# Building the one-hot picks of a GNN kernel on GpSimd, one chunk at a time behind the gathers

## The reference

```python
h_self = x @ W_self.T + b_self
messages = x[src] @ W_neigh.T + b_neigh
h_neigh = segment_sum(messages, dst, num_segments=50000)
out = layernorm(x + relu(h_self + h_neigh))      # over the last axis, eps 1e-5
```

## Time and profile before

| | us |
|---|---|
| median of three runs | 678.21 (675.71 to 680.98) |
| profiled execution, its time | 679.41 |
| its span, first to last instruction | 677.6 |
| DVE busy / of it picks | 420.5 / 104.9 |
| POOL busy / of it the 391 gathers | 406.4 / 382.0 |
| PE busy | 512.6 |
| mean granted clock of TensorE | 0.917 |

### The profile page before, as it was taken

How to read it: one execution, slowest core, us unless ns; L and a number is a source line. 1 busy time by engine, 2 the same in 40 slices (tenths; PEclk the granted TensorE clock), 3 DMA queues, 4 the chain that set the end, 5 groups by cost and what they waited for, 6 DMA issues and landing times.

```text
span 677.6 us, 12705 instructions
## 1 busy us (share of the span) xinstructions
PE 512.6 (76%) x3281; PEld 466.3 (69%) x3281; DVE 420.5 (62%) x1921; ACT 352.7 (52%) x1049; POOL 406.4 (60%) x424
## 2 busy tenths in 40 slices
PE   2045866887977978976977796978887878889883
PEld 0034756787867968866866696967776767778872
DVE  7884757587667677877557745445545543655554
ACT  1010354465655654654665655555655555656567
POOL 4776755666666665765666566566666666656610
PEclk9999897897997788999898988899999799889798
DMA  2522243354553563544544545444555454445433
GB/s 78 144 64 52 80 114 94 102 142 123 141 143 92 151 170 97 151 123 112 139 124 123 149 123 135 115 133 115 139 134 138 114 137 131 122 137 136 135 103 96
DMA packets 122942, 82.20 MB, mean 121 GB/s; under 512 B 15374, under 2 KB 115894, under 8 KB 122840
## 3 DMA queue, kind: packets, MB, share of 16 engines
q1 hardware_dynamic: 109208, 53.63, 28.4%
q0 software_dynamic: 13664, 27.77, 16.4%
HBM read 55.44 MB, written 26.71 MB: 121 GB/s over the span
## 4 chain that ended last, share of the span: by engine, by line
PE 50%; issue 20%; ACT 12%; another core or an unknown queue 6%; DVE 4%; DMA 3%; ACTq 2%; SPq 2%; POOL 1%; DVEq 0%
PE bank L890 17%; PE bank L913 11%; PE bank L914 9%; PE bank L878 6%; ACT result L1024 6%; PE bank L909 3%; ACT sums_t L997 3%; PE bank L895 3%; ACT x_t L1005 2%; DMA x_in<-in_x 2%; ACT std L1014 1%; ACTq L995 1%; DVE y L741 1%; DVE pick L731 1%
## 5 line engine op out<-in xcount | busy, mean ns | idle before, releaser
L483 POOL DMA_INDIRECT ring<-in_x,chunk_src x391 | 382.0, 977 | 229.9 <-issue 85.2
L741 DVE SCALAR_TENSOR_TENSOR y<-bank,x_in 128x384 f32<-128x384 f32 x131 | 72.5, 554 | 233.2 <-remote 114.5
L997 ACT COPY sums_t<-bank 128x192 f32 x391 | 125.2, 320 | 168.9 <-issue 45.0
L890 PE MATMUL bank<-pick,ring 128*128 128x193 f32 (+1 forms) x782 | 188.9, 370 | 10.6 <-DMA ring<-in_x,chunk_src 6.3
L913 PE MATMUL bank<-wsum_t,x_t 128*128 128x128 f32 (+1 forms) x782 | 175.7, 307 | 3.6 <-issue 3.6
L914 PE MATMUL bank<-wn_t,sums_t 128*128 128x128 f32 (+1 forms) x782 | 162.0, 290 | 7.1 <-issue 7.0
L1024 ACT ACTIVATE result<-y,minus_mean,rstd 128x128 f32<-128x128 f32 x391 | 162.9, 482 | 0.0
L890 PEld LDWEIGHTS bank<-pick,ring 128*128 128x128 f32 x782 | 142.2, 216 | 13.0 <-issue 12.7
L913 PEld LDWEIGHTS bank<-wsum_t,x_t 128*128 128x128 f32 (+1 forms) x782 | 126.8, 203 | 29.1 <-issue 29.0
L878 PE MATMUL bank<-identity,x_in 128*128 128x128 f32 x391 | 74.2, 304 | 92.5 <-issue 46.4
L914 PEld LDWEIGHTS bank<-wn_t,sums_t 128*128 128x128 f32 (+1 forms) x782 | 128.3, 206 | 8.5 <-issue 8.5
(11 more groups left out here) (118 smaller groups left out, 175.1 us busy)
## 6 DMA issues: line engine op xcount, KB each, us to landing
x_in<-in_x SPq DMA_DIRECT2D x130, 192.0 KB
out<-result SPq DMA_DIRECT2D x130, 192.0 KB
ring<-in_x,chunk_src POOLq DMA_INDIRECT x391
degrees_t<-degrees_dram SPq DMA_DIRECT2D x130, 2.2 KB
dst_padded<-in_dst SPq DMA_DIRECT2D x1, 390.6 KB
src_padded<-in_src SPq DMA_DIRECT2D x1, 390.6 KB
edge_src<-in_src SPq DMA_DIRECT2D x1, 390.6 KB
edge_dst<-in_dst SPq DMA_DIRECT2D x1, 390.6 KB
```

What stands on the lines that cost most here:

```text
L483: nc.gpsimd.indirect_dma_start(ring[:, c % RING, :], None, x, bass.IndirectOffsetOnAxis(ap=chunk_src[:, c:c + 1], axis=0)).then_inc(gather ...
L741: v.scalar_tensor_tensor(y[tau % DEEP][0:rows, 0:tiles, :], h_bank[b][0:rows, 0:tiles * DIM].rearrange("p (q d) -> p q d", q=tiles), 0.0, ...
L890: ins = mm(into[:, frame:frame + SPAN + carried], ring[:, c % RING, :], pick[tau % DEEP][:, c % TRIO, 0:SPAN + carried], start=(c == 0), s ...
L997: nc.scalar.copy(sums_t[:, bass.ds(at, SPAN)], sum_bank[c // PAIR % SUM_BANKS][:, frame:frame + SPAN]).then_inc(sums_placed, 1)
```

## The change

The picks move from DVE to POOL. POOL builds pick c - 1 right after it has issued gather c, and the last one behind the last gather. The buffers become a ring of 12 single picks, and pick c has the same place in it as its rows have in `ring`, so the wait of a gather for its place frees both. `pick_built` now counts chunks instead of trios, and PE waits for it before each chunk. A pick needs `local`, so DVE counts `locals_known` up where it finishes a part of it, and POOL waits for that. On DVE `build_picks` and its calls are gone; the three portions of the first degrees, which stood between the early picks, follow each other.

```diff
-    pick = [sb(f"pick{i}", [P, TRIO, SPAN + 2]) for i in range(DEEP)]
+    pick = sb("pick", [P, RING, SPAN + 2])
...
-            pool.wait_ge(chunks_known, 1)
-            for c in range(SPREAD):
+            def build_pick(c):
+
+                pool.wait_ge(locals_known, min((c + 1) // SPREAD, 2) + 1)
+                nc.gpsimd.tensor_scalar(pick[:, c % RING, :], columns[:], local[:, c:c + 1], None, ALU.is_equal).then_inc(pick_built, 1)
+
+            for c in range(CHUNKS):
+                if c == 0:
+                    pool.wait_ge(chunks_known, 1)
+                if c == SPREAD:
+                    pool.wait_ge(chunks_known, 3)
+                if c == 2 * SPREAD:
+                    pool.wait_ge(chunks_known, 5)
                 gather(c)
-            pool.wait_ge(chunks_known, 3)
-            for c in range(SPREAD, 2 * SPREAD):
-                gather(c)
-            pool.wait_ge(chunks_known, 5)
-            for c in range(2 * SPREAD, CHUNKS):
-                gather(c)
-
+                if c >= 1:
+                    build_pick(c - 1)
+            build_pick(CHUNKS - 1)
...
-                link(v.scalar_tensor_tensor(local[:, r0:r1], carry[:, r0:r1], float(SPAN), local[:, r0:r1], ALU.mult, ALU.max))
+                v.scalar_tensor_tensor(local[:, r0:r1], carry[:, r0:r1], float(SPAN), local[:, r0:r1], ALU.mult, ALU.max).then_inc(locals_known, 1)
...
-            def build_picks(tau):
-
-                if tau >= DEEP:
-                    dve.wait_ge(chunks_summed, TRIO * (tau - DEEP + 1))
-                for c in chunks_of(tau):
-                    ins = v.tensor_scalar(pick[tau % DEEP][:, c % TRIO, :], columns[:], local[:, c:c + 1], None, ALU.is_equal)
-                ins.then_inc(pick_built, 1)
...
-            build_picks(0)
             degrees_start(0, 1)
-            degrees_bits(0, 1, range(0, 3))
-            build_picks(1)
-            degrees_bits(0, 1, range(3, 6))
-            build_picks(2)
-            degrees_bits(0, 1, range(6, SHIFT_BITS))
+            degrees_bits(0, 1, range(0, SHIFT_BITS))
             degrees_end(0, 1)
-            built = 3
...
-                while built * TRIO < sums_ahead(t + 1):
-                    build_picks(built)
-                    built += 1
...
+                pe.wait_ge(pick_built, c + 1)
                 if c % TRIO == 0:
-                    pe.wait_ge(pick_built, tau + 1)
                     pe.wait_ge(gathered[tau % GATHER_SEMS], gathers_upto(tau))
...
-                ins = mm(into[:, frame:frame + SPAN + carried], ring[:, c % RING, :], pick[tau % DEEP][:, c % TRIO, 0:SPAN + carried],
+                ins = mm(into[:, frame:frame + SPAN + carried], ring[:, c % RING, :], pick[:, c % RING, 0:SPAN + carried],
```

## The result

| | before | after |
|---|---|---|
| median of four runs, us | 678.9 | 867.8 |
| ratio after / before | | 1.275 (1.271 to 1.279) |
| profiled execution's span, us | 677.6 | 866.6 |
| first and last gather start, us | 38.1, 648.6 | 38.4, 841.5 |
| mean step from gather to gather, us | 1.565 | 2.059 |

The kernel became 27.5% slower. I had forecast 719 us, 6% slower, with a range that ended at 775. The direction came out, and so did the mechanism, that POOL becomes the pace; the size did not.

The account below looks back on a forecast made before the run. It took PE, ACT and DVE's loop as the pace, POOL close behind. POOL's step became 1.26 + 0.43 = 1.69 us; 38.1 + 659.1 + 2.9 + 18.2 = 718.3, then + 1.8 - 1.2 = 719 us, range 672 to 775.

Parts of the forecast that it names:

- The 0.29 us a chunk: POOL's true waiting for a full ring of 12, about 112 us in all, taken as all the room POOL has.
- The line 59.8 + 390 steps: Total time in us: 59.8 for start, landing, tail and median's offset, plus 390 POOL steps from gather to gather.
- The start: Time before the first gather on POOL, expected to stay at 38.1 us.
- DVE's relief: Removing 391 picks, 104.9 us of DVE busy time; credited at 0, at best some us.
- the price x of a pick on POOL: Time one pick adds to POOL's step behind each gather: 0.43 us, the middle of 0.26 and 0.62.
- The upper bound: Highest price of a pick on POOL: DVE's 0.324 us plus a second 0.30 us gap, 0.62 us.
- Rival 4: Pick on POOL costs over 0.55 us, by double hand-over or slower compare; 793 us at 0.62; chance 0.13.
- The bound from below: Lowest price of a pick on POOL, from iota over the same 128x194: about 0.26 us.
- the gather gets shorter: POOL's gather with its gap falls from 1.277 to 1.26 us, half of 12 us of stretching credited.
- the loop of PE, ACT and DVE: Said to set the mean pace before the change, a little slower than POOL's 1.28 us a chunk.
- (2): Pick fits into the 0.30 us gap behind each POOL gather, costing 0 to 0.15 us: 675 to 682 us; chance 0.15.
- (3): DVE was part of the pace-setting loop, so removing its picks makes the kernel faster: 653 to 670 us; chance 0.10.

Follow-up runs that it names:

- `e2_no_picks`: Kernel before, with DVE building only the picks of the first six trios, reused for all later chunks: 678.8 us, ratio 0.998.
- `e4_third`: Kernel before, with POOL building the third pick of each trio of chunks and DVE the other two: 678.2 us, ratio 0.998.
- `e1_pool_load`: Kernel before, all picks still on DVE, with POOL doing the same instruction behind each gather into a ring nobody reads: 874.7 us, ratio 1.287.
- the zoo: Kernel before plus one spare POOL instruction behind each gather, another form every 30 chunks; only durations count, e.g. tensor_scalar 0.325 us at two columns.
- `e5_no_gathers`: Kernel before, with no gathers after the first 12 chunks and no PE waits for later rows: 528.0 us, ratio 0.786.

## Why the prediction was wrong

**Right: what POOL has room for.** The 0.29 us a chunk was read from the gathers' rate and the waits. A third of the picks (0.27 us) and the memset (0.14 us) cost nothing; half of them (0.4 us) made it 7% slower.

**Right: POOL becomes the pace, and where to look.** Ring waits fell from 144 to 8 us, gathers came evenly, and POOL rose to 87% (I said 78). DVE fell to 346 us busy, where I had subtracted the picks in full and said 315. The line 59.8 + 390 steps gives 863 us with the measured step of 2.059, against 868. The start held. Behind the last gather came 25.1 us (841.5 to 866.6) where I had 21.1, because the last sum came 7.7 us after it and not 2.9.

**Right: DVE's relief is worth 0**, in `e2_no_picks` and `e4_third`. Where POOL sets the pace it may be worth a little: with the picks still on DVE (`e1_pool_load`) POOL's step was 2.073 us and not 2.059, 5 us over 390 steps, hardly more than the noise.

**Wrong, the step that failed: the price x of a pick on POOL.** I took 0.43 us between bounds of 0.26 and 0.62. It is 2.059 - 1.26 = 0.80 us, so 390 x 0.37 = 144 us of the 149 that I missed by. The upper bound was no bound. It was DVE's 0.324 us plus a second gap of 0.30, as if POOL could not be slower at the arithmetic than DVE; but the gap did not double (0.04 + 0.17 us in all, less than the one gap of before), and POOL needs 2.6 times as long as DVE for the instruction (828 against 324 ns). Rival 4, "a dear pick", is what came true: x over 0.55, "by a compare that goes slower than DVE's". I gave it 0.13 and followed it only to x = 0.62 and 793 us, so the range was cut on the side where it mattered. The bound from below came from iota, which writes and does not read, and the zoo shows that it says nothing of `tensor_scalar`: same engine, same shape, 0.317 against 0.8 us.

The estimate by the Trainium skill (GPSIMD Engine Reference, section 3.1) fell with it: 0.42 us by about 1.8 cycles an element. The trace disagrees; 2.7 ns a column is 3.2 cycles at 1.2 GHz, and 0.3 us is fixed. Its advice in section 4.1, elementwise work to VectorE, is what this case bears out, and it spoke for the slow side of my range.

**Wrong: the gather gets shorter.** I credited 1.277 to 1.26 us for DVE's picks gone. It had 0.04 us in front of the pick, 1.03 us and 0.17: with its gaps 1.24, so the sum held by chance, with a longer gather and shorter gaps than I thought.

**Wrong, without effect on the sum: the loop of PE, ACT and DVE sets the pace before.** It ran at 528 us alone. What I called a pause that "comes from the PE/ACT/DVE loop" needs the indirect DMAs, at about one each 1.57 us, whether or not PE uses them and however few bytes they carry. A wait named "PE" is a wait for PE's signal, not proof that PE's own work is the limit.

**The rivals.** That the pick fits into the 0.30 us gap (2) was wrong by the timeline: POOL's step grew by the whole of the pick. DVE in the loop (3) was wrong by `e2_no_picks`.

## What to carry to other kernels

Work that is moved to another engine is priced by the same kind of instruction on that engine; if the trace has none, a row of another kind bounds it from below at best, and the range must reach to several times the price on the old engine (here 2.6 times). Before that, count the room of the receiving engine as its rate and not as its busy share: here it was 0.29 us of 1.565, and 0.8 us went in. And relief is worth something only on an engine that someone waits for: DVE without its picks brought 0.

## What the runs showed of the hardware

- **Indirect DMAs from POOL that follow each other closely go with late signals of PE.** At one each 1.54 to 1.57 us, PE's records run on while ACT, DVE and POOL get its increments some us late and all together. With 12 of them in all there is none of that, and 145 us less; with all 391 at 1.68 us or more there is none either. Rows that PE doesn't read (0.996) and 4 bytes for 512 (1.002) change nothing; a compute instruction in place of the DMA removes it (574 us). Ends on PE are modelled, so the trace can't tell a late signal from work of PE that ends late. Whether it is their descriptors, their semaphore updates or something in how they are issued stays open; a direct DMA from the same queue wasn't tried.
- **POOL's instructions differ threefold by kind at one shape.** Over 128x194 f32: memset 0.278, iota 0.317, copy 0.390, tensor_tensor 0.607, tensor_scalar 0.78 to 0.84 us.
- **POOL's instructions slow DVE's down.** DVE's pick took 425 ns beside POOL's `tensor_scalar`, 370 beside its memset, 324 beside the gathers alone and 307 without them. This agrees with the Trainium skill (SBUF — State Buffer, "Who interferes with whom"): a `tensor_scalar` of DVE that uses the second pair of ports waits for a GpSimd instruction that holds it. No run here tells which mode DVE was in.
- **A starved PE is also a slower PE.** The mean granted clock fell to 0.801, and a matmul of the products from 307 to 361 ns in the mean; the clock has two levels, 1.2 and 2.4 GHz, so the mean says (1 - 0.801) / 0.5 = 40% of the span at the lower one, against 17% before. That it cost nothing here is argued from the chain, where PE has 16% and POOL and its rows 71%; no run shows it apart. `e5_no_gathers` had 0.994.
